# The last group's stores: one semaphore for all of them, and the last store split by rows over two queues

## The chip, the cores and the metric

The kernel runs on one core of a Trainium2 chip. The metric is the device time of one execution in microseconds (us). A run's own time is a little longer than the span that its profile shows, which reaches from the first to the last instruction.

## What is computed

The reference is one graph layer with a normalisation ahead of it and a residual behind it, over 4096 nodes with 256 features, all in float32:

```
h   = max(layernorm(x), 0)            # x is 4096 x 256, over the features
agg = adj @ h                         # adj is 4096 x 4096
out = x + relu(agg @ W.T + b)         # W is 256 x 256
```

## The kernel before, in words

The kernel works on the transposed problem: features on the 128 partitions (in KB = 2 blocks), nodes along the columns. The 4096 columns are taken in 4 groups of 1024 (GROUPS, GW; the last is LAST = 3), and each group in 2 chunks of 512 columns (CHUNKS, BANK). So a group has SUMS = 4 blocks of 128 rows by 512 columns.

For each group, TensorE runs over 32 tiles of 128 nodes of adj (4 MB per group in tiles of 512 KB, loaded by SP's queue into 4 buffers) and adds up the products with h in PSUM. Each operand is split into a rounded part and a rest, so there are three passes (line 421). ScalarE makes the rounded part, VectorE the rest. Then the group's sums go through the product with W (function `w_product`, line 463), and VectorE turns each block into the output in `out_sb` by one instruction at line 320, `make_out`, which also adds x + b. It counts each block on the semaphore `s_sum`.

In groups 0 to 2 all this lies beside the sums of the next group, and POOL's queue stores each group's whole output, 1024 KB at once (line 221, semaphore `s_out`). In the last group nothing follows. There the function `pieces` cuts the fourth block in two halves of 256 columns, so that VectorE makes five pieces: three of 512 columns (256 KB each) and two of 256 columns (128 KB each). SP waits for each piece and stores it:

```
for i, (c, o, a, b) in enumerate(pieces(LAST)):
    sp.wait_ge(s_sum, LAST * SUMS + i + 1)
    at = LAST * GW + c * BANK
    sp.dma_start(out_v[:, o, at + a:at + b], out_sb[:, o, within(c, a, b)]).then_inc(s_last[i], 16)
for s in s_last:
    sp.wait_ge(s, 16)
```

Each store has a semaphore of its own in the list `s_last`, and SP ends with five waits, one for each (line 183). In the compiled program waits may share an instruction, or ride on the next instruction of the queue. When SP is through, the engines meet at the end of the block (line 53 of the profile) and the program ends. ScalarE issues no transfers in this kernel; its last work is the rounding of the last group's sums (line 390).

Of the kernel before, what the change touches and what calls it, by code (L numbers as in the profile page):

```python
# [4 lines left out]
P = 128  # L5


def bass_preln_gnn_residual(
# [20 lines left out]
    BANK = 512  # L29
    CHUNKS = 2  # L30
    GW = CHUNKS * BANK
    GROUPS = N // GW
    LAST = GROUPS - 1
    SUMS = KB * CHUNKS
# [14 lines left out]
    out_v = out_t.rearrange("(o p) i -> p o i", p=P)  # L49
# [3 lines left out]
    with ctx:  # L53
        def sb(name, shape, dt=fp32):
            return ctx.enter_context(nc.sbuf_tensor(name, shape, dt))

        def sem(name):
            return ctx.enter_context(nc.semaphore(name))
# [13 lines left out]
        out_sb = sb("out_sb", [P, KB, GW])  # L72
# [39 lines left out]
        s_xb = sem("x_plus_b_made")  # L112
        s_sum = sem("out_made")
        s_out = sem("out_stored")
        s_last = [sem(f"out_stored_last{i}") for i in range(SUMS + 1)]

        block = ctx.enter_context(nc.Block())

        def bank(g, block_, c):
            return banks[(g % 2) * SUMS + c * KB + block_]  # L120
# [3 lines left out]
        def chunk(c):  # L124
            return slice(c * BANK, (c + 1) * BANK)

        def x_piece(t):
            return next(i for i, (a, b) in enumerate(X_PIECES) if a <= t < b)
# [5 lines left out]
        def made_tile(n):  # L134
            return made_chunk(n, CHUNKS - 1) if n < EARLY else CHUNKS * EARLY + n - EARLY + 1

        def pieces(g):

            whole = [(c, o, 0, BANK) for c, o in GROUP_BANKS]
            if g < LAST:  # L140
                return whole
            c, o, _, _ = whole.pop()
            return whole + [(c, o, 0, BANK // 2), (c, o, BANK // 2, BANK)]

        def within(c, a, b):
            return slice(c * BANK + a, c * BANK + b)

        def product(g, c, o, a, b):

            return bank(g if a == 0 else g + 1, o, c)[:, a:b]  # L150

        def load_x(engine, i):
            a, b = X_PIECES[i]
            engine.dma_start(x_sb[:, a:b, :], x_v[:, a:b, :]).then_inc(s_x[i], 16)

        @block.sync
        def _(sp):
            def load_chunk(t, c):
                sp.dma_start(adj_in[:, t, chunk(c)], adj_v[:, t, chunk(c)]).then_inc(s_early[t][c], 16)

            def load_adj(n):
                g, t = divmod(n, TILES)
                if n >= U:
                    sp.wait_ge(s_hi, made_tile(n - U))
                    sp.wait_ge(s_lo, made_tile(n - U))
                sp.dma_start(adj_in[:, n % U, :], adj_v[:, t, g * GW:(g + 1) * GW]).then_inc(s_adj[n % U], 16)


            load_x(sp, 0)
            load_chunk(0, 0)  # L170
            load_chunk(0, 1)
            load_chunk(1, 0)
            load_chunk(1, 1)
            for n in range(EARLY, GROUPS * TILES):
                load_adj(n)

            sp.wait_ge(s_out, 16 * LAST)
            for i, (c, o, a, b) in enumerate(pieces(LAST)):
                sp.wait_ge(s_sum, LAST * SUMS + i + 1)
                at = LAST * GW + c * BANK  # L180
                sp.dma_start(out_v[:, o, at + a:at + b], out_sb[:, o, within(c, a, b)]).then_inc(s_last[i], 16)
            for s in s_last:
                sp.wait_ge(s, 16)

        @block.gpsimd
        def _(pool):
            for i in range(1, U):
                load_x(pool, i)
# [18 lines left out]
            for t in range(TILES):  # L207
                root(t)
                if t == 0:
                    load_x(pool, U)  # L210
                i = t // U + U + 1
                if t % U == 2 and i < len(X_PIECES):
                    load_x(pool, i)
                if t == 7:
                    pool.dma_start(w_sb[:], wt_v).then_inc(s_w, 16)
                    pool.dma_start(b_sb[:], b_cols).then_inc(s_b, 16)
# [117 lines left out]
        @block.scalar  # L334
        def _(act):
            def adj_rounded(n):
                k = n % U

                act.wait_ge(s_adj[k], 16 * (n // U + (k >= EARLY)))
                if n >= U:  # L340
                    act.wait_ge(s_pe, n - U + 1)
                nc.scalar.activation(adj_hi[:, k, :], adj_in[:, k, :], ACT.Copy).then_inc(s_hi, 1)  # L342

            def early_rounded(t, c):
                act.wait_ge(s_early[t][c], 16)
                nc.scalar.activation(adj_hi[:, t, chunk(c)], adj_in[:, t, chunk(c)], ACT.Copy).then_inc(s_hi, 1)  # L346

            def h_rounded(t):
                k = t % U
                act.wait_ge(s_rstd, t + 1)  # L350
                act.wait_ge(s_centred, t + 1)
                nc.scalar.activation(h_sb[:, t, 0, :], centred[:, k, :], ACT.Copy,  # L352
                                     scale=rstd[:, k:k + 1]).then_inc(s_hhi, 1)

            def centre(t):
                k = t % U
                act.wait_ge(s_x[x_piece(t)], 16)
                act.wait_ge(s_neg, t)
                if t >= U:

                    act.wait_ge(s_hlo, t - U + 1)
                nc.scalar.activation(centred[:, k, :], x_sb[:, t, :], ACT.Relu, bias=neg_mean[:, k:k + 1]  # L362
                                     ).then_inc(s_centred, 1)


            nc.scalar.activation(scratch[:], nc.const_aps.tensor(1.0, [P, 1], fp32), ACT.Copy)
            h_rounded(0)
            early_rounded(0, 0)
            early_rounded(0, 1)
            centre(1)  # L370
            early_rounded(1, 0)
            h_rounded(1)
            early_rounded(1, 1)
            for t in range(EARLY, TILES):
                centre(t)
                adj_rounded(t)
                h_rounded(t)

            act.wait_ge(s_w, 16)
            nc.scalar.activation(w_hi[:], w_sb[:], ACT.Copy).then_inc(s_whi, 1)  # L380

            def sums_rounded(g):
                if g >= 1:
                    act.wait_ge(s_prod, g * SUMS)
                if g < LAST:
                    act.wait_ge(s_pe, (g + 1) * TILES)
                for i, (c, kb) in enumerate(GROUP_BANKS):
                    if g == LAST:
                        act.wait_ge(s_chunk, c + 1)
                    nc.scalar.activation(agg_hi[:, kb, chunk(c)], bank(g, kb, c)[:], ACT.Copy  # L390
                                         ).then_inc(s_ahi, 1)

            def add_bias(g):

                act.wait_ge(s_xt, 16 * (g + 1))
                for c, o in GROUP_BANKS:
                    nc.scalar.activation(xt_sb[:, o, chunk(c)], xt_sb[:, o, chunk(c)],  # L397
                                         ACT.Identity, bias=b_sb[:, o:o + 1]).then_inc(s_xb, 1)

            act.wait_ge(s_b, 16)  # L400
            for g in range(1, GROUPS):
                for t in range(TILES):
                    if t == SPLIT_AT:
                        sums_rounded(g - 1)
                    if t == OUT_AT:
                        add_bias(g - 1)
                    adj_rounded(g * TILES + t)
            add_bias(LAST)
            sums_rounded(LAST)

        @block.tensor
        def _(pe):
# [112 lines left out]
```

## Time and profile before

| what | value |
|---|---|
| median of 3 runs | 380.95 us (380.69 to 380.96) |
| the profiled execution | 380.8 us |
| its span | 379.0 us |
| TensorE busy in the span | 375.1 us (99%) |
| granted TensorE clock | 1.00 of full speed |
| last output piece made by VectorE | 376.21 us, taking 0.48 us |
| from there to the end of the span | 2.3 us |

TensorE is busy nearly all the time. Behind its last product stand one VectorE instruction, the last store, and the program's end. The 1.8 us between the span and the execution's own time lie outside what the profile shows.

### The profile page before, as it was taken

The page shows a single profiled execution, that of the slowest core. Times are in us where ns is not written, and L with a number is a line of the kernel's source. Part 1 is how long each engine was busy: PE and PEld are TensorE (multiplying, and loading weights), DVE is VectorE, ACT ScalarE, POOL GpSimd, SP SyncE. Part 2 cuts the span into 40 slices and gives each one's busy share as a digit, 9 for nine tenths or more (in the row PEclk, how much of TensorE's full clock was granted, in tenths as well). Part 3 has the DMA queues.
Part 4 walks back from the last instruction along what each step waited for, and adds up shares of the span by engine and source line. Part 5 has one row for each costly group of instructions (what it writes and reads, how often), then busy time and mean ns, then how long its engine had stood idle before and what let it go on. Part 6 is the DMA issues. An engine that isn't in the chain of part 4 may idle for free.

```text
span 379.0 us, 4516 instructions
## 1 busy us (share of the span) xinstructions
PE 375.1 (99%) x1651; PEld 308.1 (81%) x1651; DVE 212.2 (56%) x294; ACT 181.8 (48%) x228; POOL 50.1 (13%) x88
## 2 busy tenths in 40 slices
PE   8999999999999999999999999999999999999997
PEld 4888888888888888888888888888888888888885
DVE  5999988874744453535564544444464444444424
ACT  5888776764443434343643343433355243434341
POOL 5687732320010000000001000000000100000000
PEclk9999999999999999999999999999999999999999
DMA  7989877577659565655566856565656775555203
GB/s 263 369 301 304 275 256 258 185 235 256 210 186 317 174 215 178 208 177 209 176 206 207 294 178 209 178 205 184 201 189 195 256 242 195 187 202 185 92 2 111
DMA packets 22774, 80.25 MB, mean 212 GB/s; under 512 B 2496, under 2 KB 2880, under 8 KB 22752
## 3 DMA queue, kind: packets, MB, share of 16 engines
q1 hardware_dynamic: 19584, 68.30, 54.1%
q0 software_dynamic: 3168, 11.67, 8.6%
q8 instruction: 13, 0.21, 0.2%
q14 instruction: 9, 0.07, 0.0%
HBM read 75.76 MB, written 4.19 MB: 211 GB/s over the span
## 4 chain that ended last, share of the span: by engine, by line
PE 98%; DMA 1%; DVE 0%; ACT 0%; POOL 0%; issue 0%; POOLq 0%
PE bank L421 92%; PE bank L463 6%; DMA x_sb<-x_dram 1%; ACT adj_hi L346 0%; POOL rstd L204 0%; ACT h_sb L352 0%; DVE out_sb L320 0%; DVE stats L240 0%; DVE mean_var L245 0%; DVE var_eps L249 0%; POOLq L200 0%
## 5 line engine op out<-in xcount | busy, mean ns | idle before, releaser
L421 PE MATMUL bank<-adj_hi,h_sb 128*128 128x512 f32 x1024 | 254.3, 389 | 0.2 <-ACT adj_hi L346 0.2
L229 DVE TENSOR_TENSOR adj_lo<-adj_in,adj_hi 128x1024 fp32r<-128x1024 f32 x126 | 154.6, 1227 | 145.7 <-ACT adj_hi L342 145.5
L421 PEld LDWEIGHTS bank<-adj_hi,h_sb 128*128 128x128 f32 x1024 | 192.0, 188 | 40.5 <-issue 0.5
L342 ACT ACTIVATE adj_hi<-adj_in 128x1024 fp32r<-128x1024 f32 x126 | 133.5, 1060 | 176.7 <-PE bank L421 174.5
L421 PE MATMUL bank<-adj_lo,h_sb 128*128 128x512 f32 x512 | 137.5, 389 | 0.0
L421 PEld LDWEIGHTS bank<-adj_lo,h_sb 128*128 128x128 f32 x512 | 96.1, 188 | 20.0
L204 POOL TENSOR_TENSOR rstd<-var_eps,minus_half 128x1 f32<-128x1 f32 x32 | 30.5, 954 | 3.4 <-DVE var_eps L249 0.8
L221 POOL DMA_DIRECT2D out_t_dram<-out_sb x3 | 2.2, 726 | 211.0 <-DVE out_sb L320 211.0
L352 ACT ACTIVATE h_sb<-centred,rstd 128x256 fp32r<-128x256 f32 x32 | 16.0, 499 | 3.6 <-POOL rstd L204 3.2
L362 ACT ACTIVATE centred<-x_sb,neg_mean 128x256 f32<-128x256 f32 x31 | 15.5, 500 | 2.1 <-DVE neg_mean L264 1.9
L270 DVE SCALAR_TENSOR_TENSOR h_sb<-centred,rstd,h_sb 128x256 fp32r<-128x256 f32 x32 | 15.3, 477 | 1.0 <-ACT h_sb L352 1.0
L240 DVE BATCH_NORM_STATS2 stats<-x_sb 128x6 f32<-128x256 f32 x32 | 13.4, 418 | 3.0 <-DMA x_sb<-x_dram 3.0
L309 DVE TENSOR_TENSOR agg_lo<-bank,agg_hi 128x512 fp32r<-128x512 f32 x16 | 10.0, 683 | 7.8 <-ACT agg_hi L390 7.8
L320 DVE SCALAR_TENSOR_TENSOR out_sb<-bank,minus_b,xt_sb 128x512 f32<-128x512 f32 (+1 forms) x17 | 11.4, 714 | 4.7 <-ACT xt_sb L397 3.7
L463 PE MATMUL bank<-agg_lo,w_hi 128*128 128x512 f32 (+1 forms) x34 | 12.8, 376 | 0.0
L463 PE MATMUL bank<-agg_hi,w_lo 128*128 128x512 f32 (+1 forms) x34 | 12.8, 376 | 0.0
L463 PE MATMUL bank<-agg_hi,w_hi 128*128 128x512 f32 (+1 forms) x34 | 12.8, 376 | 0.0
L198 POOL TENSOR_TENSOR var_eps<-mean_var,eps_sb 128x1 f32<-128x1 f32 x31 | 7.4, 237 | 31.7 <-DVE mean_var L245 31.3
L390 ACT ACTIVATE agg_hi<-bank 128x512 fp32r<-128x512 f32 x16 | 8.3, 596 | 6.2 <-PE bank L421 6.2
L397 ACT ACTIVATE xt_sb<-xt_sb,b_sb 128x512 f32<-128x512 f32 x16 | 10.2, 708 | 0.0
L463 PEld LDWEIGHTS bank<-agg_lo,w_hi 128*128 128x128 f32 x34 | 6.4, 188 | 1.2
L463 PEld LDWEIGHTS bank<-agg_hi,w_hi 128*128 128x128 f32 x34 | 6.4, 188 | 1.2
(25 smaller groups left out, 42.7 us busy)
## 6 DMA issues: line engine op xcount, KB each, us to landing
adj_in<-adj_t_dram SPq DMA_DIRECT2D x126, 512.0 KB, 3.6
xt_sb<-x_t_dram POOLq DMA_DIRECT2D x4, 1024.0 KB, 7.4
x_sb<-x_dram POOLq DMA_DIRECT2D x7, 512.0 KB, 6.5
out_t_dram<-out_sb POOLq DMA_DIRECT2D x3, 1024.0 KB, 4.9
adj_in<-adj_t_dram SPq DMA_DIRECT2D x4, 256.0 KB, 4.8
out_t_dram<-out_sb SPq DMA_DIRECT2D x3, 256.0 KB, 2.0
x_sb<-x_dram POOLq DMA_DIRECT2D x3, 128.0 KB, 4.6
w_sb<-w_t_dram POOLq DMA_DIRECT2D x1, 256.0 KB, 6.0
```

The costliest lines, as they stand in the source:

```text
L204: nc.gpsimd.tensor_tensor(rstd[:, k:k + 1], var_eps[:, k:k + 1], minus_half[:], ALU.pow).then_inc(s_rstd, 1)
L229: nc.vector.tensor_tensor(adj_lo[:, k, :], adj_in[:, k, :], adj_hi[:, k, :].bitcast(fp32), ALU.subtract).then_inc(s_lo, 1)
L240: nc.vector.bn_stats(stats[:, k, :], x_sb[:, t, :]).then_inc(s_stats, 1)
L270: nc.vector.scalar_tensor_tensor(out=h_sb[:, t, 1, :], in0=centred[:, k, :], scalar=rstd[:, k:k + 1], in1=h_sb[:, t, 0, :].bitcast(fp32), ...
L309: nc.vector.tensor_tensor(agg_lo[:, kb, chunk(c)], bank(g, kb, c)[:], agg_hi[:, kb, chunk(c)].bitcast(fp32), ALU.subtract).then_inc(s_alo, 1)
L320: nc.vector.scalar_tensor_tensor(out=out_sb[:, o, cols], in0=product(g, c, o, a, b), scalar=minus_b[:, o:o + 1], in1=xt_sb[:, o, cols], op ...
L342: nc.scalar.activation(adj_hi[:, k, :], adj_in[:, k, :], ACT.Copy).then_inc(s_hi, 1)
L352: nc.scalar.activation(h_sb[:, t, 0, :], centred[:, k, :], ACT.Copy, scale=rstd[:, k:k + 1]).then_inc(s_hhi, 1)
L362: nc.scalar.activation(centred[:, k, :], x_sb[:, t, :], ACT.Relu, bias=neg_mean[:, k:k + 1]).then_inc(s_centred, 1)
L397: nc.scalar.activation(xt_sb[:, o, chunk(c)], xt_sb[:, o, chunk(c)], ACT.Identity, bias=b_sb[:, o:o + 1]).then_inc(s_xb, 1)
L421: last = nc.tensor.matmul(bank(g, kb, c)[:], h_sb[:, t, hp, kb * P:(kb + 1) * P], adj_parts[ap][:, n % U, chunk(c)], start=(t == 0 and (hp ...
L463: last = nc.tensor.matmul(product(g, c, o, a, b), (w_hi, w_lo)[wp][:, kb, o * P:(o + 1) * P], (agg_hi, agg_lo)[ap][:, kb, within(c, a, b)] ...
```

## The change

The five semaphores of the last group's stores become one, on which SP waits once for the whole count. The first four stores stay as they are on SP's queue. The fifth piece (256 columns, 128 KB) is stored in two halves of 64 rows: SP's queue takes rows 0 to 63, and ScalarE's queue takes rows 64 to 127, behind a wait for the same piece.

```diff
-        s_last = [sem(f"out_stored_last{i}") for i in range(SUMS + 1)]
+        s_last = sem("last_group_stored")
...
+        def store_last(engine, piece, rows):
+            c, o, a, b = piece
+            at = LAST * GW + c * BANK
+            engine.dma_start(out_v[rows, o, at + a:at + b], out_sb[rows, o, within(c, a, b)]
+                             ).then_inc(s_last, 16)
...
             sp.wait_ge(s_out, 16 * LAST)
-            for i, (c, o, a, b) in enumerate(pieces(LAST)):
+            for i, piece in enumerate(pieces(LAST)):
                 sp.wait_ge(s_sum, LAST * SUMS + i + 1)
-                at = LAST * GW + c * BANK
-                sp.dma_start(out_v[:, o, at + a:at + b], out_sb[:, o, within(c, a, b)]).then_inc(s_last[i], 16)
-            for s in s_last:
-                sp.wait_ge(s, 16)
+
+                store_last(sp, piece, slice(0, P if i < SUMS else P // 2))
+
+            sp.wait_ge(s_last, 16 * (SUMS + 2))
...
             add_bias(LAST)
             sums_rounded(LAST)
+            act.wait_ge(s_sum, LAST * SUMS + SUMS + 1)
+            store_last(act, pieces(LAST)[-1], slice(P // 2, P))
```

## Rows read from the trace of the kernel before

**Rows 1.** The page's heading and busy times.

```profile
span 379.0 us, 4516 instructions
PE 375.1 (99%) x1651; PEld 308.1 (81%) x1651; DVE 212.2 (56%) x294; ACT 181.8 (48%) x228; POOL 50.1 (13%) x88
```

**Rows 2.** The chain that ended last, its end: start us, us, what.

```profile
294.51 76.16 PE bank L421 x336
370.67 5.52 PE bank L463 x30
376.19 0.02 issue
376.21 0.48 DVE out_sb L320
```

**Rows 3.** Timeline of SP's queue in four short stretches: start us, us.

```profile
374.21 0.34 SPq L181 DMA_DIRECT2D out_t_dram<-out_sb  x1
...
375.56 0.33 SPq L181 DMA_DIRECT2D out_t_dram<-out_sb  x1
...
376.01 1.05 SPq L181 DMA_DIRECT2D out_t_dram<-out_sb  x2
...
376.73 0.33 SPq L181 DMA_DIRECT2D out_t_dram<-out_sb  x1
```

**Rows 4.** The stores of line 181: duration ns min/median/max, then time to landing.

```profile
L181 SPq DMA_DIRECT2D out_t_dram<-out_sb x5: 332/344/358, 373.4 to 376.7; - x5
...
DMA to landing us min/median/max: 1.8/2.0/2.1
```

**Rows 5.** Transfers from 377.4 to 378.4 us, in 40 slices of 0.025 us.

```profile
DMA  8976422677959899897985642100000000000000
GB/s 287 328 206 205 123 82 82 205 246 246 410 205 451 287 410 451 287 369 246 451 287 165 205 164 82 41 0 0 0 0 0 0 0 0 0 0 0 0 0 0
```

**Rows 6.** Transfers from 374.3 to 375.3 us, in 40 slices of 0.025 us.

```profile
DMA  6689689699948968968996775200002948949966
GB/s 246 246 328 655 246 328 573 246 410 492 410 164 328 655 246 328 655 246 328 328 573 246 246 246 164 82 0 0 0 0 82 410 164 328 655 164 410 573 246 246
```

**Rows 7.** What SP's queue waited for near the end: us, times, longest.

```profile
SPq L183 <- DMA out_t_dram<-out_sb: 1.4, 2, 1.0
SPq L53 <- PEq L53: 0.2, 1, 0.2
```

**Rows 8.** The waits of line 183: duration ns, first and last start us.

```profile
L183 SPq EVENT_SEMAPHORE  x2: 28/28/28, 378.1 to 378.5; - x2
```

**Rows 9.** The block's end, line 53, same columns.

```profile
L53 ACTq DRAIN  x1: 1117/1117/1117, 370.7 to 370.7; - x1
...
L53 SPq COMPARE_BRANCH  x1: 38/38/38, 378.6 to 378.6; - x1
L53 SPq DRAIN  x1: 7/7/7, 378.8 to 378.8; - x1
L53 SPq EVENT_SEMAPHORE  x1: 17/17/17, 378.9 to 378.9; - x1
```

**Rows 10.** ScalarE's last work in the timeline: start us, us.

```profile
370.70 1.09 ACT L390 ACTIVATE agg_hi<-bank 128x512 fp32r<-128x512 f32 x2 [4.29 <-PE bank L421]
```

**Rows 11.** Transfers by line: KB each, median us from issue to landing.

```profile
x_sb<-x_dram POOLq DMA_DIRECT2D x3, 128.0 KB, 4.6
...
out_t_dram<-out_sb SPq DMA_DIRECT2D x2, 128.0 KB, 1.9
x_sb<-x_dram SPq DMA_DIRECT2D x1, 128.0 KB, 2.2
```

**Rows 12.** The issues of line 154, by queue: duration ns min/median/max.

```profile
L154 POOL DMA_DIRECT2D x_sb<-x_dram x10: 537/586/688, 1.3 to 56.6; - x10
L154 SPq DMA_DIRECT2D x_sb<-x_dram x1: 381/381/381, 0.7 to 0.7; - x1
```

## The prediction

> **What bounds the kernel now.** I read the page's busy times first. TensorE is busy for 375.1 of 379.0 us [rows 1], so the first thing to see is how little lies outside it. The chain that ended last says where: TensorE's products run to 376.19, one VectorE instruction of 0.48 us makes the fifth output piece, and the chain's listing ends at 376.69 [rows 2]. From there to the end at 379.0 are 2.3 us, and these are all that the change touches. Nothing that it edits runs before the first store of the last group, so TensorE's 370 us ahead of it stay as they are.
>
> Next I took those 2.3 us apart, from SP's queue, the transfers in short slices, and the waits:
>
> - 376.73: SP issues the fifth store, which takes 0.33 us of its queue [rows 3]. So the queue starts 0.04 us behind VectorE's end at 376.69, and it isn't late from the fourth store: that was issued at 376.01, and an issue of 0.36 us at most [rows 4] leaves the queue free from 376.37 on.
> - 377.58: the fifth store's first data. In the slices the traffic falls to a tenth or two of its usual rate at 377.50 to 377.58 and then comes up again [rows 5]. I read this dip as the end of store four and the start of store five. It gives a lead of 377.58 - 376.73 = 0.85 us from issue to data. A second place agrees: the store issued at 374.21 [rows 3] has its first data after an empty stretch, in the slice at 375.05 [rows 6], a lead of 0.84 us.
> - 378.05: the last data; from there all slices are empty [rows 5]. So 128 KB took 0.47 us.
> - 378.5: the landing, 1.8 us behind the issue [rows 4], and the second wait of line 183 begins there [rows 8]. So some 0.45 us pass between the last data and the moment at which SP sees the count.
> - 378.6: the branch at the block's end, then the drain at 378.8 and the meeting of the engines at 378.9 [rows 9].
>
> The lead, the data, the receipt and the program's end thus share the tail as 0.85 + 0.47 + 0.45 + 0.5 us. Only the second, the smallest but one, is carrying bytes.
>
> **The change part by part.**
>
> *One semaphore in place of five.* The five waits stand in the trace as two instructions of line 183 [rows 8] and the branch behind them [rows 9], which I take to carry the fifth. The first of the two begins at 378.1, when store four lands, and hides in the wait for store five: SP waits for landings twice, 1.4 us in all and 1.0 the longer, from the last issue's end at 377.06 [rows 7, 3]. The second begins at 378.5, when store five lands, and the branch comes at 378.6. With a single wait the branch itself can carry it, as it seems to carry one now, and would begin at 378.5. Gain: one instruction of 28 ns with its dispatch, 0.1 us at the resolution of these rows. Bounds: nothing (the wait stays an instruction of its own) and 0.1 us. I take 0.1. The one wait asks for all six stores, of which the first four land earlier (the fourth at 378.1), so it waits for nothing new. That several stores in flight count on one semaphore costs nothing in time, because nobody waits for a part of the count.
>
> *The first four stores.* Same engine, sizes and order: 0.
>
> *SP's half of the fifth store.* Its issue has the same place, 376.73. Every store of line 181 took 332 to 358 ns to issue, whether its rows had 1 or 2 KB [rows 4], but all of them have 128 rows, and no row here shows one of 64. The lead of 0.85 us may shrink with the rows or not. Bounds: nothing, if the lead is a fixed delay; and half of it, 0.4 us, if all of it goes with the rows, and if ScalarE's does too. The nearest rows, those for a full and a half width, say that the lead follows neither bytes nor width, so I take 0.
>
> *The data.* Still 128 KB. During the store the share of busy transfer engines is mostly 7 to 9 tenths of a slice [rows 5], so a second queue finds few idle slots: 0.47 us as a whole if both halves come together, some 0.24 us for each. Gain bound: the two or three thin slices at either side, under 0.1 us. I take 0.
>
> The Trainium skill, page "DMA: Bandwidth & Descriptors", section "Rules for kernel authors", speaks against this part: two transfers to disjoint halves of the partitions aren't worth making, since both spread over the same 16 engines and serialise. By that rule the data's 0.47 us would stay and the split would give nothing, where the intended overlap would give up to 0.24 us. The full slices above are on the rule's side. The sum takes the same side without it.
>
> *ScalarE's half.* ScalarE ends its last rounding at 371.8 [rows 10] and has drained by then [rows 9]. It stands idle for the 4.9 us before the piece is made, and nothing is queued behind its new wait but its own drain, which the meeting at 378.9 alone needs. So the issue costs no other work. What it costs the path is its lag L behind SP's half. While L is under 0.24 us, SP's half covers it and the data still end at 378.05. Beyond that they end at 377.58 + L + 0.24. No row shows ScalarE issuing a transfer, so bounds come from the other queues. Below: L = 0. In the middle: it issues only after SP's issue is through, L = 0.33 us, so the data end at 378.15, 0.1 us later. Above: it behaves as POOL's queue, whose 128 KB loads took 4.6 us to land where SP's took 2.2 [rows 11], L = 2.4 us. SP's first issue of the program took 0.38 us against a median of 0.34 later [rows 12, 4], so a first use costs a queue of SP's kind some 0.04 us. I take L below 0.24 and so 0, as it is a queue that, like SP's, only hands the store over, whereas POOL's issues take 0.54 to 0.69 us [rows 12].
>
> *Outside the span.* The 1.8 us between span and execution stay. One more queue in use may add there, four semaphores fewer may save; no row shows either, and I take 0.
>
> **The sum.** On the profiled execution: 380.8 - 0.1 (wait) + 0 (lead) + 0 (data) + 0 (ScalarE's lag) = 380.7 us, its span 378.9. That execution was 0.15 us under the median of the three runs, 380.95, so for a median I say 380.85 us. A difference counts here as measured from 0.2% on, 0.76 us; the whole stretch from VectorE's end to the end is 2.3 us, and the sum moves it by 0.1.
>
> **The rivals.**
>
> *A, forecast: the split is neutral and the wait gives 0.1.* 380.85 us, chance 0.58.
>
> *B, the two issues go one behind the other.* ScalarE's lag is then SP's 0.33 us, the data end 0.1 us later, the wait gives 0.1 back: 380.95 us. Here the split is a loss. For it: two queues issue at the same instant, which happens nowhere before. Against: nothing in the rows. The Trainium skill, page "Perfetto Trace Analysis", section "DMA Instruction — HWDGE (DVE, Sync)", has the issuer lock a shared descriptor generator, which is this case; by its rule the second issue would be longer or later by the first one's length. No row of this kernel can show it. Chance 0.22.
>
> *C, the lead shrinks with the rows.* Both halves begin 0.2 to 0.4 us sooner: 380.85 - 0.4 = 380.45 at best. For it: the lead is the largest term of the tail, and I don't know what it is made of. Against: the lead was 0.84 and 0.85 for rows of 2 KB and of 1 KB. Chance 0.09.
>
> *D, the other side: ScalarE's queue is late as POOL's is.* Its half lands 2.4 us behind SP's, with half of the data covered: 380.85 + 2.4 - 0.24 = 383.0 us, slower by 0.5%. It decides by the bound above as soon as L passes 0.76 + 0.1 + 0.24 = 1.1 us, that is, when ScalarE's half lands more than some 2.7 us behind its issue. For it: the only two queues in the trace differ by that much. Against: POOL's loads ran among the heavy traffic of the start, and POOL's issue alone is longer. Chance 0.04.
>
> *E, the third queue costs time outside the span.* Two queues and all else share 1.8 us; if that were the queues' alone, a third would be 0.9 us: 381.75. It decides over 0.86 us, so only near its upper end. Chance 0.07, half of it over the bound.
>
> **Range and chances.** A, B and C span 380.45 to 380.95, to which the spread of runs (380.69 to 380.96) adds some 0.15 at either side, and the lower part of E reaches up to 381.4. So the range is 380.3 to 381.4. Faster by over 0.2% would need 380.19 or less: C at its best together with luck, 0.03. Slower needs 381.71: D and half of E, 0.07. The rest, 0.90, is within.
>
> **What the profile after would show.** For A: SP's and ScalarE's issues both at about 376.73 behind VectorE's end, both some 0.33 us long; a landing of about 1.8 us; no wait instruction between the landing and the branch at the block's end, and the last landing to the span's end 0.4 instead of 0.5 us. For B: ScalarE's issue begins or ends 0.3 us later, and the slices show data ending near 378.15. For C: the dip in the slices moves ahead of 377.5. For D: ScalarE's store lands near 381. For E: the span is right and the time outside it is over 1.8 us. The prediction is wrong if anything before 373 us moves, since no term covers that, or if the difference between own time and span changes.

## The result, and the profile after

The changed kernel takes 381.54 us (median of 20 runs, 381.1 to 382.36), the kernel before 380.92 us (20 runs, 380.58 to 381.66). The ratio is 1.0015, 95% interval 1.0009 to 1.0021: a loss of 0.6 us, between 0.3 and 0.8. It stays within the 0.2% that the forecast called no change, but it is real, and the median lies 0.14 us above the top of the forecast's range, 381.4. The sign is wrong too: 0.1 us had been expected as a gain.

All of it must lie in the tail if the change works as its diff reads. The end of the chain in the profile after, start us, us, what:

```profile
294.44 76.16 PE bank L429 x336
370.61 5.52 PE bank L471 x30
376.13 0.03 issue
376.15 0.48 DVE out_sb L326
```

These are the rows of [rows 2] with each start 0.06 us earlier. VectorE ends at 376.63 and the span at 379.3: the tail is 2.7 us, where it was 379.0 - 376.69 = 2.3. So the profiled executions place 0.4 us behind VectorE's end. The 1.8 us outside the span stay: 381.16 us of own time for a span of 379.3.

The queues of SP and ScalarE in that tail, timeline, start us, us:

```profile
375.95 0.36 SPq L155 DMA_DIRECT2D out_t_dram<-out_sb  x1
...
376.66 0.54 SPq L155 DMA_DIRECT2D out_t_dram<-out_sb  x1
...
376.67 0.57 ACTq L155 DMA_DIRECT2D out_t_dram<-out_sb  x1
```

The two halves are issued at the same moment, 0.03 us behind VectorE's end, as planned. But each issue takes 0.54 and 0.57 us, where the whole store took 0.33 [rows 3]. Their landings, KB each, median us to landing:

```profile
out_t_dram<-out_sb SPq DMA_DIRECT2D x1, 128.0 KB, 2.0
out_t_dram<-out_sb SPq DMA_DIRECT2D x1, 64.0 KB, 2.0
out_t_dram<-out_sb ACTq DMA_DIRECT2D x1, 64.0 KB, 2.3
```

A half of 64 KB takes longer to land than the whole of 128 KB did before, 1.8 us at the least in [rows 4]. The same slices as in [rows 5], 377.4 to 378.4 us in steps of 0.025, then those from 378.1 to 378.6 us in steps of 0.0125 with the queues' shares in it:

```profile
DMA  6621000000000000006629969955976979879779
GB/s 205 205 82 41 0 0 0 0 0 0 0 0 0 0 0 0 0 0 164 164 82 246 246 164 246 328 123 123 328 164 205 288 205 369 246 164 369 164 164 246
...
DMA  9967589639999694999393693960240320210000
...
q10 hardware_dynamic: 80, 0.07, 51.9%
q1 hardware_dynamic: 34, 0.02, 16.2%
```

The gap that had been three thin slices is now fourteen empty ones: the fourth store's data end at 377.5, and the next come at 377.85, 1.19 us behind SP's issue, not 0.85. Queue 10 is ScalarE's; all its 80 packets lie behind 378.1: 64 rows and 16 packets of 4 bytes, which every store has at its end and which are called its counts here. In the stretch from 377.84 to 378.13 every packet was SP's, so ScalarE's data start 0.28 us behind SP's. They end at 378.58, 1.9 us behind the issue, against 1.4 before. (The slices count a packet where it starts. By the packet records the last store's data of before end at 378.09, not at the 378.05 that the slices of [rows 5] suggest.) What comes after is 0.76 us instead of 0.88, a little shorter, as expected. The waits and the branch at the block's end, SP's rows:

```profile
SPq L53 <- DMA out_t_dram<-out_sb: 1.7, 1, 1.7
...
L53 SPq COMPARE_BRANCH  x1: 33/33/33, 379.0 to 379.0; - x1
L53 SPq DRAIN  x1: 7/7/7, 379.1 to 379.1; - x1
L53 SPq EVENT_SEMAPHORE  x1: 17/17/17, 379.3 to 379.3; - x1
```

The branch itself waits for the landings, once, and no wait instruction stands before it as in [rows 8].

### The profile page after: what moved, and what is told of

Read it like the earlier page. It is cut to its first block, busy times and chain, and to the rows that moved or that the text cites. A ratio compares the mean times of both kernels' runs of the same rounds, so it can differ in the third digit from the quotient of the medians.

```text
span 379.3 us, 4515 instructions
## 1 busy us (share of the span) xinstructions
PE 375.3 (99%) x1651; PEld 308.1 (81%) x1651; DVE 212.0 (56%) x294; ACT 181.9 (48%) x228; POOL 50.0 (13%) x88
## 4 chain that ended last, share of the span: by engine, by line
PE 99%; DVE 0%; issue 0%
PE bank L429 92%; PE bank L471 6%; PE bank L484 1%; DVE out_sb L326 0%
```

## The experiments

"Tail" below is the span's end less VectorE's end in the profiled execution. Ratios are to the kernel before on the same chip, with their 95% interval. The one semaphore is kept everywhere but in e4. The diffs are against the changed kernel. In e7 to e11, too, all stores are SP's, so ScalarE's two lines go, and the count of the one wait is made to match. e7 and e9 to e11 were run once each (382.26, 384.89, 383.27 and 383.76 us, with nine or ten stores in the last group); only their traces are read.

### First set: which part costs

**e1, the one semaphore without the split.**

```diff
-                store_last(sp, piece, slice(0, P if i < SUMS else P // 2))
+                store_last(sp, piece, slice(0, P))
-            sp.wait_ge(s_last, 16 * (SUMS + 2))
+            sp.wait_ge(s_last, 16 * (SUMS + 1))
...
-            act.wait_ge(s_sum, LAST * SUMS + SUMS + 1)
-            store_last(act, pieces(LAST)[-1], slice(P // 2, P))
```

> One semaphore alone, the last store whole on SP's queue. Theory S (two simultaneous issues hinder each other; the one wait saves 0.1 us): the issue is back at 0.33 us, the data end 1.3 us behind it, the branch follows the landing directly, span 0.1 us under before, median 380.85 against 380.95 of before. Rival W (many stores on one semaphore are what costs): the landing comes 0.4 us later, as in the changed kernel, and the time stays near 381.5.

380.88 us, ratio 0.9998 (0.9987 to 1.0009). Its tail, from VectorE's end at 377.22 to 379.4, is 2.2 us, 0.1 less than before, as expected; the last store's issue is back at 0.33 us. A tenth of a microsecond can't be seen in the runs. Rival W is out. (VectorE ends 0.5 us later in this execution than in that of before. Its chain holds waits of ScalarE and VectorE at 10 to 12 us, so this comes from the start, not from the end that was edited; that is why tails are compared here, and not spans.)

**e2, both halves on SP's queue.**

```diff
-            sp.wait_ge(s_last, 16 * (SUMS + 2))
+            store_last(sp, pieces(LAST)[-1], slice(P // 2, P))
+            sp.wait_ge(s_last, 16 * (SUMS + 2))
...
-            act.wait_ge(s_sum, LAST * SUMS + SUMS + 1)
-            store_last(act, pieces(LAST)[-1], slice(P // 2, P))
```

> Both halves of rows issued by SP, one behind the other. Theory S: each issue takes at most 0.33 us since nobody else issues, the second begins 0.33 us or less behind the first, and the data end 0 to 0.15 us later than in one_sem: 380.85 to 381.0. Rival R (half of the rows is what costs, by slower packets or a slower issue): the packets show the same thin traffic as in the changed kernel, and the data end 0.5 us later than before: 381.4 or more.

381.71 us, ratio 1.0025 (1.0015 to 1.0035), tail 3.1 us: worse than over two queues. SP's queue, timeline, start us, us; then the transfers from 378.6 to 379.2 us, in which the first half lies alone:

```profile
377.49 0.55 SPq L155 DMA_DIRECT2D out_t_dram<-out_sb  x1
...
378.08 0.59 SPq L155 DMA_DIRECT2D out_t_dram<-out_sb  x1
...
DMA  0000019461192990599929988744032120000000
...
q1 hardware_dynamic: 80, 0.07, 45.7%
```

This run broke my theory S. SP issues both halves, no other queue issues anything, and the issues are 0.55 and 0.59 us all the same. So it isn't two issues at one moment that hinder each other; the store of 64 rows itself is slow, rival R. The second part of R can be worked out from the last row. 45.7% of 16 transfer engines over 0.6 us are 4.4 us of work for 80 packets; the 16 counts take 9 ns or so each by the packet records, so a row of 1 KB takes 66 ns. For the whole store of before, the same sum gives 48 ns (65.9% from 377.55 to 378.15 us, for 129 rows and 20 counts).

**e3, the whole last store on ScalarE's queue.**

```diff
-                store_last(sp, piece, slice(0, P if i < SUMS else P // 2))
+                if i < SUMS:
+                    store_last(sp, piece, slice(0, P))
-            sp.wait_ge(s_last, 16 * (SUMS + 2))
+            sp.wait_ge(s_last, 16 * (SUMS + 1))
...
-            store_last(act, pieces(LAST)[-1], slice(P // 2, P))
+            store_last(act, pieces(LAST)[-1], slice(0, P))
```

> The last store whole, but from ScalarE's queue; nothing else issues at that time. Theory S: its issue takes some 0.35 us and the landing 1.8 to 1.9 us as on SP's queue, so the time is that of one_sem within 0.1 us: 380.85. Rival Q (ScalarE's queue is slow by itself, or its presence costs outside the span): issue near 0.57 us, landing 2.3 us, time 381.3 to 381.5; or the time outside the span rises over 1.8 us.

381.05 us, ratio 1.0001 (0.9991 to 1.0011), tail 2.3 us. ScalarE's only transfer of the program, and its landing:

```profile
L155 ACTq DMA_DIRECT2D out_t_dram<-out_sb x1: 377/377/377, 376.6 to 376.6; - x1
...
out_t_dram<-out_sb ACTq DMA_DIRECT2D x1, 128.0 KB, 1.8
```

The queue costs 0.04 us over SP's and nothing outside the span: 1.78 us there as a median, 1.77 for the kernel before beside it. The rest of the 0.1 us over e1's tail is the wait: here the single wait stands as an instruction of its own at 378.4 us, and the branch begins 0.07 us behind the landing instead of 0.02 in e1. Rival Q is out, and with it rivals D and E of the prediction.

**e4, the change with a semaphore for each store.**

```diff
-        s_last = sem("last_group_stored")
+        s_last = [sem(f"out_stored_last{i}") for i in range(SUMS + 2)]
...
-                             ).then_inc(s_last, 16)
+                             ).then_inc(s_last[i], 16)
...
-            sp.wait_ge(s_last, 16 * (SUMS + 2))
+            for s in s_last:
+                sp.wait_ge(s, 16)
```

> The split over two queues with a semaphore for each of the six stores. Theory S: as the changed kernel, both issues near 0.55 us, plus the 0.1 us of the waits at the end: 381.6. Rival W (the shared semaphore costs): the landing is back at 1.8 us and the time near 380.95.

381.56 us, ratio 1.0012 (1.0002 to 1.0022), tail 2.8 us, issues of 0.55 and 0.57 us. So the split alone is the loss, and the shared semaphore has no part in it.

### Second set: two queues, two issues, or 64 rows

**e5, halves by columns on two queues.** Each half has 128 rows by 128 columns.

```diff
+        last_c, last_o, last_a, last_b = pieces(LAST)[-1]
+        last_mid = (last_a + last_b) // 2
+        left = (last_c, last_o, last_a, last_mid)
+        right = (last_c, last_o, last_mid, last_b)
...
-                store_last(sp, piece, slice(0, P if i < SUMS else P // 2))
+                if i < SUMS:
+                    store_last(sp, piece, slice(0, P))
+                else:
+                    store_last(sp, left, slice(0, P))
...
-            store_last(act, pieces(LAST)[-1], slice(P // 2, P))
+            store_last(act, right, slice(0, P))
```

> The last store split by columns instead of rows: 128 rows by 128 columns each, one on SP's and one on ScalarE's queue at the same moment. Theory F (a store of 64 rows is a slow form: issue 0.55 us, first data 1.19 us behind it, thin traffic): with 128 rows both issues are back at 0.33 to 0.38 us, the lead at 0.85 to 0.9 us, and the tail from VectorE's end to the end of the span at 2.2 to 2.3 us, so 380.9 us. Rival B (simultaneous issues stand in each other's way): one of the two issues, or its first data, comes 0.3 us later all the same.

380.97 us, ratio 0.9995 (0.9986 to 1.0004), tail 2.2 us. Timeline, start us, us:

```profile
377.37 0.33 SPq L155 DMA_DIRECT2D out_t_dram<-out_sb  x1
...
377.38 0.37 ACTq L155 DMA_DIRECT2D out_t_dram<-out_sb  x1
```

Two queues at one moment, and each issue is as short as alone. Rival B is wrong about the issue. It keeps a part: by the packet records ScalarE's data begin 0.17 us behind SP's, more than the 0.04 us by which its issue is longer. The data of the two together last 0.59 us, those of the whole store in e3 0.51, and the tail is that of e1, so nothing is won.

**e6, the same halves by columns, both on SP** (the store of `right` stands behind that of `left` on SP, and ScalarE's two lines go).

> The same two halves of columns, both issued by SP. Theory F: the second issue ends at 0.70 us behind the first's begin, its data come 0.35 to 0.4 us behind the first half's, and the tail is 2.19 + 0.37 - 0.25 = 2.3 us: 380.95 to 381.05. Rival N (any second store costs what the second half of rows cost): tail near 3.1 us, 381.7.

381.1 us, ratio 0.9999 (0.999 to 1.0008), tail 2.5 us. The issues are 0.33 and 0.45 us: one that stands right behind another takes 0.1 us more. I had put the tail at 2.3; 0.1 of the miss is that. Rival N, a second store as such, would have given 3.1.

**e7, stores by parts of rows**, all on SP:

```diff
+        ROW_PARTS = [[(0, 64), (64, 128)], [(0, 96), (96, 128)], [(0, 128)], [(0, 128)],
+                     [(32, 96), (0, 32), (96, 128)]]
...
-                store_last(sp, piece, slice(0, P if i < SUMS else P // 2))
+                for rows in ROW_PARTS[i]:
+                    store_last(sp, piece, slice(*rows))
```

> Stores by parts of rows, all on SP: piece 1 as 0-63 and 64-127, piece 2 as 0-95 and 96-127, pieces 3 and 4 whole, piece 5 as 32-95, 0-31, 96-127. Theory F1 (any count under 128 takes the slow issue): 0.55 us or more for every part, 0.34 for the whole ones. F2 (issue grows with the descriptors left over, so fewer rows are cheaper): 32 rows issue faster than 64, 96 slower. For the thin traffic: if it comes from 64 neighbouring rows lying on one half of the memory's ports, then rows 32 to 95 carry their 64 KB in some 0.25 us; if it comes from the form, in 0.45 us as rows 0 to 63 did.

The issues fit neither F1 nor F2: rows 0-63, 64-127 and 32-95 took 0.57 us each, but 96-127 took 0.43 and 0.42, and 0-95 and 0-31 took 0.58. All but the first and the seventh stood behind another issue, so the order was in the way; that made the third set necessary. The traffic tells more. Transfers from 378.5 to 378.84 us, when rows 32 to 95 were on the way, with the last few packets of the whole store before them until 378.57:

```profile
DMA packets 70, 0.05 MB, mean 157 GB/s; under 512 B 18, under 2 KB 70, under 8 KB 70
...
q1 hardware_dynamic: 70, 0.05, 47.1%
```

47.1% of 16 engines over 0.34 us are 2.6 us for 52 rows and 18 counts, 46 ns for a row, and by the packet records none took over 51. That is the speed of the whole store, for a store of 64 rows of 1 KB that as rows 0 to 63 or 64 to 127 needs 66. But those began on idle transfer engines, and rows 32 to 95 behind another store. The nearest case of 64 neighbouring rows behind another store is in e10 below, rows 0 to 63 from 380.02 to 380.38 us:

```profile
q1 hardware_dynamic: 68, 0.06, 59.4%
```

With 54 rows and 14 counts that is 61 ns for a row. In the last stores of e9 (rows 0 to 63) and e11 (64 to 127) it was some 49 and 55 ns by the packet records. All three have packets of 70 ns and more. So a start behind another store helps, but the 46 ns of rows 32 to 95 is still the lowest and the only even one: which rows are taken matters, though one store of rows 32 to 95 is all that shows it. The Trainium skill, page "SBUF — State Buffer", section "Door 1: The DMA port swizzle", says why that may be: partitions 0 to 63 lie on 8 of the memory's 16 ports and 64 to 127 on the other 8. Rows 32 to 95 lie half in one set and half in the other. The measurement agrees; the ports themselves aren't seen in a trace.

**e8, a narrower last store**, as a candidate for a faster version: e1 with the fourth block cut at 384 columns.

```diff
-            return whole + [(c, o, 0, BANK // 2), (c, o, BANK // 2, BANK)]
+            return whole + [(c, o, 0, BANK * 3 // 4), (c, o, BANK * 3 // 4, BANK)]
```

> One semaphore, all stores on SP, the fourth block cut in 384 and 128 columns instead of 256 and 256. Under every theory: the last store carries 64 KB in 0.25 instead of 0.5 us, VectorE's last instruction takes 0.35 instead of 0.48 us but may start 0.1 to 0.2 us later, behind the one of 384 columns. From the end of TensorE's last product to the span's end 0.1 to 0.25 us less than in one_sem, 380.75 us; within the spread of the runs.

380.95 us, ratio 0.9996 (0.9988 to 1.0005). From the end of TensorE's last product (377.04 here, 376.71 in e1) to the span's end are 2.6 us against 2.7 in e1 and 2.8 before. VectorE goes from the 384 columns to the 128 without a pause, so it has become the next limit. The gain in the trace, 0.15 us before rounding, is within what I expected, and the runs can't tell it from nothing.

### Third set: which stores are slow to issue

Each kernel issues four partial stores with SP's queue empty, and the rest behind the last piece. The edit of e9; e10 and e11 have other entries:

```diff
+            ALONE = {0: (0, 32), 1: (32, 64), 3: (96, 128), 4: (64, 128)}
...
+                if i in ALONE:
+                    store_last(sp, piece, slice(*ALONE[i]))
+            for i, a, b in REST:
+                store_last(sp, pieces(LAST)[i], slice(a, b))
```

> Four partial stores, each issued with SP's queue empty: rows 0-31 of piece 1, 32-63 of piece 2, 96-127 of piece 4, 64-127 of piece 5; the rest behind the end. Theory K (any count of rows other than 128 takes the slow issue, and the short ones of the run before were short only for standing behind another): all four near 0.55 us. Theory L (it depends on which rows): rows 96-127 near 0.33 us, the others near 0.55 us.

> As before, with rows 0-95, 32-127, 0-15 and 64-95. Theory K: all near 0.55 us. Theory L: those that reach row 127 near 0.33 us, the others near 0.55 us (but rows 64-127 were 0.57 us, which speaks against it). Theory M (the time goes with the number of rows): 16 rows least, 96 rows most.

> As before, with rows 0-111, 112-127, 0-119 and 0-63. Theory K: all near 0.55 us, the last as measured alone before. Theory L: rows 112-127 near 0.33 us. Theory M: 16 rows least, 120 rows most.

Issues on an empty queue of SP, in us:

| rows | issue | kernels |
|---|---|---|
| 128 | 0.33 to 0.36 | all |
| 112, 120 | 0.36, 0.38 | e11 |
| 96 (0-95, 32-127) | 0.35 to 0.36, 0.34 | e10, e12 |
| 64 (0-63, 64-127, 32-95) | 0.54 to 0.57 | after, e2, e4, e7, e9, e11 |
| 32 (0-31, 32-63, 64-95, 96-127) | 0.36, 0.34, 0.31, 0.32 | e9, e10 |
| 16 (0-15, 112-127) | 0.32, 0.33 | e10, e11 |

Two rows of e9's timeline, one of e10's and three of e11's, start us, us: rows 96-127 and, on the next piece, rows 64-127; then rows 64-95; then rows 112-127, the form 0 to 119, and what stands behind the 64 rows of e11:

```profile
376.49 0.32 SPq L155 DMA_DIRECT2D out_t_dram<-out_sb  x1
...
377.15 0.55 SPq L155 DMA_DIRECT2D out_t_dram<-out_sb  x1
```

```profile
376.48 0.31 SPq L155 DMA_DIRECT2D out_t_dram<-out_sb  x1
```

```profile
374.48 0.33 SPq L155 DMA_DIRECT2D out_t_dram<-out_sb  x1
...
376.33 0.38 SPq L155 DMA_DIRECT2D out_t_dram<-out_sb  x1
...
377.60 0.57 SPq L155 DMA_DIRECT2D out_t_dram<-out_sb  x1
```

All three theories fall. It isn't every count but 128, not the rows' place, and not their number in order. Of the counts tried, only 64 rows are slow, whichever they are. The first data follow the same line: by the packet records they come 1.20 us behind the issue for the 64 rows of e9 and e11, and 0.81 to 0.86 us behind it for 16, 32, 96, 112 and 120 rows. The issue right behind a store of 64 rows is long too (0.57 here for 16 rows, 0.58 in e7 for 0-31 and 0-95), which clears up e7. Where a store of 64 rows stood itself right behind another issue the time varied: 0.47 us twice in e9 and once in e11, 0.55 in e10, 0.57 in e7 behind another of 64 rows. Why just 64, no run tells.

**e12, the change with its cut at row 96.**

```diff
-                store_last(sp, piece, slice(0, P if i < SUMS else P // 2))
+                store_last(sp, piece, slice(0, P if i < SUMS else 3 * P // 4))
...
-            store_last(act, pieces(LAST)[-1], slice(P // 2, P))
+            store_last(act, pieces(LAST)[-1], slice(3 * P // 4, P))
```

> The changed kernel with the last store cut at row 96 instead of 64: SP takes rows 0-95, ScalarE rows 96-127. Theory H (a store of just 64 rows holds the issue for 0.55 us; 32 and 96 rows don't): issues of 0.33 to 0.36 on SP and 0.35 to 0.38 us on ScalarE, leads near 0.85 and 1.0 us, and the tail from VectorE's end to the span's end is 2.2 to 2.35 us instead of 2.7; the median 380.9 to 381.1. Rival B again (rows split over two queues at the same moment cost the 0.4 us in themselves): tail near 2.7 us, 381.4 to 381.6.

381.13 us, ratio 1.0008 (0.9999 to 1.0017), tail 2.5 us: between the two. The issues, and the traffic from 377.9 to 378.7 us:

```profile
377.08 0.35 SPq L155 DMA_DIRECT2D out_t_dram<-out_sb  x1
...
DMA  0345982799907987895899597866834411100000
...
q1 hardware_dynamic: 117, 0.10, 48.2%
q10 hardware_dynamic: 48, 0.03, 12.6%
```

Theory H is right in its first half: with 96 and 32 rows the issues are 0.35 and 0.40 us, and SP's data begin 0.85 us behind the issue. Its tail was put too low by 0.1 us or more. The data now last 0.7 us instead of 0.5, for SP's 96 rows are slow too: 62 ns for a row of 1 KB. ScalarE's data begin 0.31 us behind SP's, though its store has 32 rows, so its lag isn't a matter of 64 rows. Its rows took 46 ns each, scattered among SP's, where the same rows 96 to 127 alone took 59 in e7 and e9. So the long issue and lead of 64 rows are one part of the loss, the data's longer stretch is another, and a cut elsewhere heals only the first. How the second divides between slow rows and ScalarE's lag, no run separates.

## Why the prediction was wrong

*What bounds the kernel, and where the change can act:* right. All of the 0.4 us lies behind VectorE's end, and tail and runs agree over the kernels that were run eleven times or more: tails of 2.2 to 2.3 us go with ratios of 0.9995 to 1.0001, 2.5 with 0.9999 and 1.0008, 2.7 and 2.8 with 1.0015 and 1.0012, and 3.1 with 1.0025. The runs give 0.6 us for the change, 0.3 to 0.8, so they don't say whether more than the tail's 0.4 is in it; the range's top was missed by 0.14 us.

*The one semaphore:* right, 0.1 us (e1, and the branch that waits itself).

*SP's half, the lead:* this is the step that failed first. I took 0 and bounded it by nothing and a gain of 0.4 us, since wide and narrow stores had the same lead. It is a loss of 0.34 us: 1.19 instead of 0.85, of which 0.21 is the issue itself. All the rows that I used had 128 partitions, and I said so, but I let the unknown point only one way. A bound on the side of a loss was missing, and nothing in the rows spoke against one.

*The data:* the second failure. I counted 0.24 us for each half. Each takes 0.45 (377.85 to 378.30 and 378.13 to 378.58), almost as long as the whole store's 0.47 to 0.5, at 63 to 67 ns for a row instead of 48. The full slices of [rows 5] rightly told that a second queue finds little room; they couldn't tell that each row would take longer in a store of half the rows.

*ScalarE's lag:* taken as 0, measured 0.28 us (0.17 in e5, 0.31 in e12). That is within its bounds and near the 0.33 us of rival B, and with halves of 0.24 us it would indeed have cost nearly nothing: the step "while L is under 0.24, SP's half covers it" fell with the data's term.

The sum with what was measured, on the profiled executions: 2.3 + 0.34 (lead) + 0.28 (lag) + 0.45 - 0.5 (data) - 0.1 (wait) - 0.05 (receipt, 0.4 instead of 0.45) = 2.7 us. That is the tail.

*The rivals.* B, with chance 0.22, had the sign of the split right and nearly the size of ScalarE's lag, 0.33 against 0.28 us. But it priced the split at 0.1 us, as it had neither the longer lead nor the slower rows, and its reason doesn't show: e5's two issues run at the same time, each as short as alone. By the lock that the Trainium skill describes ("Perfetto Trace Analysis", section "DMA Instruction — HWDGE (DVE, Sync)"), one of two simultaneous issues would be longer by the other's length. They aren't, though something that is shared may be behind the 0.17 to 0.31 us by which ScalarE's data lag; its cause is open. D and E are refuted by e3. C is refuted too: even with 16 and 32 rows the lead is 0.81 to 0.86 us. The rule of the Trainium skill, page "DMA: Bandwidth & Descriptors", section "Rules for kernel authors", against splits by partition halves held, and the case goes beyond it: the split isn't just useless, it costs (a tail of 2.7 instead of 2.3 us).

## What to carry to other kernels

At the end of a kernel like this one, keep the last store in one transfer over all 128 rows. If it must be cut, cut columns over two queues: that cost nothing here. Over one queue columns cost 0.3 us against e1, and rows cost 0.4 us over two queues and 0.8 over one against the kernel before. When an edit gives an operation a shape that no row of the trace has, let its price go both ways: fewer rows was slower per row and slower to issue. And a tail of 2.3 us, of which 0.5 carries bytes, has little to win; four semaphores saved at its end were worth 0.1 us, under what 12 runs can show.

## What the runs showed of the hardware

- A store of 64 rows takes 0.54 to 0.57 us to issue on SP and 0.57 on ScalarE; stores of 16, 32, 96, 112, 120 and 128 rows take 0.31 to 0.38 us on SP. The first data come 1.19 to 1.20 us behind SP's issue instead of 0.81 to 0.86. The store right behind one of 64 rows takes 0.57 to 0.59 us. The cause is open.
- A row of 1 KB takes 48 ns in a store of 128 rows, 46 in one of rows 32 to 95, 66 in one of rows 0 to 63, and 62 in one of rows 0 to 95. Rows 96 to 127 took 59 ns alone and 46 scattered among another queue's packets (e12). So it depends on which rows are taken, and also on what goes on beside them.
- ScalarE's queue, unused until then, issued a store in 0.38 us and landed it in 1.8 us, with nothing added outside the span (e3). Where SP issued at the same moment, ScalarE's data came 0.17 to 0.31 us behind SP's (after, e5, e12).
- An issue that stands right behind another takes 0.1 us more (0.45 after 0.33 us in e6; 0.41 to 0.45 in e7 to e10 where no store of 64 rows is near; but 0.34 for 8 rows in e11).
